# Three accumulation tables in the filter stage, their clearing moved to the setup, and list work of the setup moved

## What is computed

```python
edge_index = jnp.stack([src, dst])
x = _layernorm(x + _L0_gnn_ref(x, edge_index, edge_weight, W, b))            # two hops of normalised sums over edges
x = _layernorm(x + _L1_gnn_ref(x, ..., edge_attr_3, edge_index))             # attention, segment softmax by dst
x = _layernorm(x + _L2_gnn_ref(x, edge_attr_64, src, dst, ...))              # attention, segment softmax by dst
x = _layernorm(x + _L3_gnn_ref(x, edge_attr_20, ..., edge_index))            # filter

def _L3_gnn_ref(x, rbf, Wf1, bf1, Wf2, bf2, Wu1, bu1, Wu2, bu2, gamma, beta, ei):
    row, col = (ei[0], ei[1])                        # row is src: unsorted
    filt = silu(rbf @ Wf1 + bf1) @ Wf2 + bf2
    agg = jax.ops.segment_sum(x[col] * filt, row, num_segments=x.shape[0])
    h = silu(agg @ Wu1 + bu1) @ Wu2 + bu2
    return x + batch_norm(h)                         # over all nodes
```

## Time and profile before

| what | value |
|---|---|
| median of three runs | 7849.68 us (7843.85 to 7850.1) |
| the profiled execution, its own time | 7853.95 us |
| its span | 7852.0 us |
| busy share of the span: PE, DVE, ACT, POOL | 53%, 77%, 46%, 46% |
| bytes moved by DMA, mean rate | 1765 MB, 225 GB/s |
| setup | 0 to 628 us |
| hop 0, hop 1 | 628 to 1150, 1150 to 1681 us |
| layer 0, attention 1, layer 1 | to 2533, to 3610, to 4238 us |
| attention 2, layer 2 | to 4965, to 5602 us |
| filter, update, finish | to 6572, to 7345, to 7852 us |

### The profile page before, as it was taken

How to read it: one execution, slowest core, us unless ns; L and a number is a source line. 1 busy time by engine, 2 the same in 40 slices (tenths; PEclk the granted TensorE clock), 3 DMA queues, 4 the chain that set the end, 5 groups by cost and what they waited for, 6 DMA issues and landing times. The chain is left out here.

```text
span 7852.0 us, 84021 instructions
## 1 busy us (share of the span) xinstructions
PE 4153.3 (53%) x18168; PEld 3161.6 (40%) x18168; DVE 6030.9 (77%) x18094; ACT 3581.2 (46%) x9619; POOL 3600.6 (46%) x3559
## 2 busy tenths in 40 slices
PE   7910000039999333335886222000498998999644
PEld 4500000038888222223554222000266666888522
DVE  7896657767776899998998777899888885554676
ACT  4505750038888333334775000234444443444688
POOL 7806767764443333334555555000266662000477
PEclk9955555569999555557998555555699999999755
DMA  9028989978787566667998888677677776666799
GB/s 285 1 6 236 313 295 298 299 252 243 243 243 227 201 220 220 217 219 249 341 342 276 263 264 264 223 251 252 174 114 115 114 113 147 203 203 204 242 316 304
DMA packets 1120799, 1765.08 MB, mean 225 GB/s; under 512 B 227356, under 2 KB 586372, under 8 KB 1120170
## 3 DMA queue, kind: packets, MB, share of 16 engines
q1 hardware_dynamic: 683786, 1019.20, 40.7%
q0 software_dynamic: 188768, 422.51, 21.9%
q10 hardware_dynamic: 247744, 318.00, 11.7%
HBM read 969.63 MB, written 840.95 MB: 231 GB/s over the span
## 5 line engine op out<-in xcount | busy, mean ns | idle before, releaser
L1125 POOL DMA_INDIRECT rows<-T,index_i x784 | 759.4, 969 | 884.2 <-DVE sums L1267 698.5
L817 ACT ACTIVATE xo<-z,shift,rsd 128x256 f32<-128x256 f32 x1568 | 849.8, 593 | 0.4 <-issue 0.2
L1635 POOL DMA_INDIRECT xt<-X,node_i x392 | 370.8, 946 | 908.4 <-POOLq L1702 784.6
L1386 POOL DMA_INDIRECT A<-comb,ai x392 | 617.6, 1575 | 340.4 <-DMA A<-comb,ai 227.1
L1142 PE MATMUL psE<-encs,attr 4*128 4x256 f32 x784 | 369.7, 649 | 635.5 <-DMA attr<-in_attr3T 633.3
L879 POOL DMA_INDIRECT xt<-in_x,input_i x392 | 375.2, 957 | 470.6 <-DVE xb L894 394.2
L766 PE MATMUL psC<-sums,chainT 128*128 128x256 f32 x4 | 2.4, 700 | 1100.6 <-PEq L655 1100.6
L1401 PE MATMUL psH<-rbf,wf1s 20*128 20x256 f32 x784 | 228.4, 411 | 644.7 <-DMA rbf<-in_rbfT 644.7
L789 DVE BATCH_NORM_STATS2 row_stats<-z 128x6 f32<-128x256 f32 x1568 | 564.5, 402 | 0.1
L1142 PEld LDWEIGHTS psE<-encs,attr 4*128 4x128 f32 x784 | 243.9, 326 | 760.9 <-DMA attr<-in_attr3T 702.2
L801 ACT ACTIVATE sd<-mean_var,epsc 128x2 f32<-128x2 f32 x784 | 237.9, 303 | 584.8 <-DVE mean_var L796 583.0
(11 more groups left out here) (358 smaller groups left out, 14805.5 us busy)
## 6 DMA issues: line engine op xcount, KB each, us to landing
X<-xo ACTq DMA_DIRECT2D x588, 256.0 KB, 3.6
S<-sums SPq DMA_DIRECT2D x196, 544.0 KB, 2.8
st<-S SPq DMA_DIRECT2D x392, 272.0 KB, 4.2
S<-sums SPq DMA_DIRECT2D x392, 256.0 KB, 4.0
A<-zero SPq DMA_DIRECT2D x196, 512.0 KB
T<-tt ACTq DMA_DIRECT2D x196, 280.0 KB
rowsd<-T SPq DMA_DIRECT2D x98, 560.0 KB
T<-tt ACTq DMA_DIRECT2D x196, 272.0 KB
```

The lines of the kernel that those rows point to most:

```text
L817: ins = e.activation(y[s][:, k, :], z[s][:, k, :], ACT.Identity, bias=shift[s][:, k, :], scale=rsd[s][:, k, :])
L1125: e.indirect_dma_start(rows[s][:, k, :], None, table, bass.IndirectOffsetOnAxis(ap=at_i[:, c:c + 1], axis=0))\
L1386: e.indirect_dma_start(A[k], bass.IndirectOffsetOnAxis(ap=ai[s][:, k, :], axis=0), comb[s][:, k, :], None, compute_op=ALU.add).then_inc(si ...
L1635: e.indirect_dma_start(xt[s][:, k, :], None, X3, bass.IndirectOffsetOnAxis(ap=node_i[:, c:c + 1], axis=0))\
```

## The change

What it does, in four parts:

1. A third table A2. The adds of the filter go to A0, A1, A2 in turn by the column's number q, and each waits for add q - 3. `update_nodes` loads all three and adds twice.
2. The attentions no longer store zeros, and wait for none. In block 1 of the setup SP issues, behind the copy to `XT`, 294 stores of zeros (98 for each table, 512 KB each) from a tile `wide_zero` whose rows are 4 KB. At the end of block 4 SP waits for them all.
3. `compress` of the list FREE is cut into pieces and put on DVE between the columns of the histogram, one piece before every 17th column. What it needs is made ahead of the histogram: the scan `frees`, and its sum over earlier partitions by one small product on PE.
4. The shifts to the right of `expand(FREE)`, `input_i`, `head_i`, `tail_i` and `turn_i` are put on DVE in the second hop, one piece after every eighth step for the first twelve. The two fetches of `brow` are at the head of POOL's queue in that hop.

The diff, cut to its core:

```diff
-    A = [dram("A0", NP + P, D), dram("A1", NP + P, D)]
+    A = [dram(f"A{t}", NP + P, D) for t in range(3)]
...
                         e.dma_start(XT[:, 0:D], x.rearrange("p c d -> (p c) d")).then_inc(widened, 16)
+                        for t in A:
+                            for c in range(0, C, QZ):
+                                e.dma_start(nodes(t)[:, c:c + QZ, :], wide_zero[:].rearrange("p (c d) -> p c d", c=QZ)).then_inc(emptied, 16)
...
                         e.memset(zero[:], 0.0).then_inc(zeroed, 1)
+                        e.memset(wide_zero[:], 0.0).then_inc(zeroed, 1)
...
+                        def list_free(t):
+                            if t == 0:
+                                locate(e, link, FREE)
+                                distance(e, link, FREE, notfirst, frees)
+                            elif t <= BITS:
+                                mirror_bit(e, link, BITS - t)
+                            elif t == BITS + 1:
+                                place(e, link, FREE, notfirst)
+                            elif t <= 2 * BITS + 1:
+                                shift_left(e, link, FREE, t - BITS - 2)
+
+                        EVERY = C // (2 * BITS + 3)
...
                         def one_hot(i, s):
+                            if (i * NS + s) % EVERY == EVERY - 1:
+                                list_free((i * NS + s) // EVERY)
...
-                        locate(EMPTY)
-                        locate(FREE)
+                        own(FREE)
+                        locate(e, link, EMPTY)
                         e.sem_inc(located, 1)
-                        compress(FREE, notfirst, frees)
-                        own(FREE)
-                        compress(EMPTY, empty, empties)
+                        distance(e, link, EMPTY, empty, empties)
...
                         join(2)
                         expand(FREE, 2)
-                        link(e.tensor_tensor(ids[:], ids[:], notfirst[:], ALU.mult))
...
                     @block.sync
                     def _(e):
                         e.wait_ge(tabled, 1)
                         e.wait_ge(widened, 16)
                         e.dma_start(nodes(XT)[:, :, D:XW], degs[:]).then_inc(placed, 16)
                         e.wait_ge(placed, 16)
+                        e.wait_ge(emptied, 16 * len(A) * (C // QZ))
...
+                        def list_rows(i, s):
+                            t, rest = divmod(i * NS + s, 8)
+                            if rest == 7 and t < 10:
+                                shift_right(e, link, 9 - t)
+                            elif rest == 7 and t == 10:
+                                inputs_of_rows(e, link)
+                            elif rest == 7 and t == 11:
+                                e.wait_ge(bounded, 32)
+                                turns_of_rows(e, link)
...
-                        unrolled(R, NS, [(mix, 0), (add, 0)] if hop else [(weigh, 0), (square, 0), (weight, 0), (add, 2)])
+                        unrolled(R, NS, [(mix, 0), (add, 0), (list_rows, 0)] if hop else [(weigh, 0), (square, 0), (weight, 0), (add, 2)])
...
-                        written(N, NS, ([(take, 0)] if layer == 1 else []) + [(stage, 0), (store, 2), (empty, 2)])
+                        written(N, NS, ([(take, 0)] if layer == 1 else []) + [(stage, 0), (store, 2)])
...
-                                hold(e, *done(added[k], i, s, 1))
-                                e.indirect_dma_start(A[k], bass.IndirectOffsetOnAxis(ap=ai[s][:, k, :], axis=0), comb[s][:, k, :], None,
-                                                     compute_op=ALU.add).then_inc(signal(added[k], s), 16)
+                                q = (i * NS + s) * G + k
+                                hold(e, *landed(q - len(A)))
+                                e.indirect_dma_start(A[q % len(A)], bass.IndirectOffsetOnAxis(ap=ai[s][:, k, :], axis=0), comb[s][:, k, :], None,
+                                                     compute_op=ALU.add).then_inc(added[q % len(A)], 16)
...
                             e.dma_start(more[s][:], nodes(A[1])[:, c, :]).then_inc(signal(loaded, s), 16)
+                            e.dma_start(third[s][:], nodes(A[2])[:, c, :]).then_inc(signal(loaded, s), 16)
...
                             hold(e, *done(loaded, i, s))
+                            e.tensor_tensor(more[s][:], more[s][:], third[s][:], ALU.add).then_inc(signal(paired, s), 1)
+                            hold(e, *done(paired, i, s))
                             e.tensor_tensor(agg[s][:], agg[s][:], more[s][:], ALU.add).then_inc(signal(summed, s), 1)
```

More of the change, by code:

```diff
@@ L136, in build @@
         isfirst, notfirst, islast, notlast, follows = [sb(n, [P, C]) for n in ("isfirst", "notfirst", "islast", "notlast", "follows")]
+        codes, other, moved = [sb(n, [P, 2, 2 * C]) for n in ("codes", "other", "moved")]
+        rowid, dst_f, brow, carried_r = sb("rowid", [P, C]), sb("dst_f", [P, C]), sb("brow", [P, 2, XW]), sb("carried_r", [P, C])
         head_i, tail_i, start_e = sb("head_i", [P, 1], I32), sb("tail_i", [P, 1], I32), sb("start_e", [P, 1], I32)
@@ L171, in setup @@
                 assert W <= 1024 and C < 512
-                rowid, free, empty, frees, empties = [tmp(n, [P, C]) for n in ("rowid", "free", "empty", "frees", "empties")]
+                empty, frees, empties = [tmp(n, [P, C]) for n in ("empty", "frees", "empties")]
+                EMPTY, FREE, BITS = 0, 1, 10
+                rem, rev, bit, near2, rowsC = tmp("rem", [P, C]), tmp("rev", [P, C]), tmp("bit", [P, C]), tmp("near2", [P, P]), tmp("rowsC", [P, P])
+                pk0, pk1, ck0 = [[tmp(f"{n}{j}", [P, 1]) for j in range(2)] for n in ("pk0", "pk1", "ck0")]
@@ new lines, in setup, with locate @@
+                oh = [[tmp(f"oh{j}{h}", [P, P]) for h in range(2)] for j in range(2)]
+                listed = [tmp(f"listed{j}", [P, W]) for j in range(2)]
+                def locate(e, link, j):
+                    link(e.tensor_scalar(near2[:], rowsC[:], below[:, j:j + 1], None, ALU.is_le))
+                    link(e.tensor_reduce(pk1[j][:], near2[:], AX, ALU.add))
+                    link(e.tensor_scalar(pk0[j][:], pk1[j][:], -1.0, None, ALU.add))
+                    link(e.tensor_scalar(oh[j][0][:], rows0[:], pk0[j][:], None, ALU.is_equal))
+                    link(e.tensor_scalar(oh[j][1][:], rows0[:], pk1[j][:], None, ALU.is_equal))
+                    link(e.scalar_tensor_tensor(ck0[j][:], pk0[j][:], -float(C), below[:, j:j + 1], ALU.mult, ALU.add))
@@ new lines, in place, with shift_left @@
+                def place(e, link, j, flag):
+                    link(e.tensor_scalar(rev[:], rev[:], CODE, 1.0, ALU.mult, ALU.add))
+                    link(e.tensor_tensor(rev[:], rev[:], cols[:], ALU.add))
+                    link(e.memset(listed[j][:, 0:C], 0.0))
+                    link(e.tensor_tensor(listed[j][:, C:W], rev[:], flag[:], ALU.mult))
+                def shift_left(e, link, j, b):
+                    d, top = 2 ** b, CODE * 2 ** (BITS - 1 - b)
+                    a, z = (listed[j][:], other[:, 0, :]) if b % 2 == 0 else (other[:, 0, :], listed[j][:])
+                    e.tensor_scalar(moved[:, 0, :], a, top, 0.0, ALU.subtract, ALU.max)
+                    link(e.scalar_tensor_tensor(z, a, top, a, ALU.is_lt, ALU.mult))
+                    link(e.tensor_tensor(z[:, 0:W - d], z[:, 0:W - d], moved[:, 0, d:W], ALU.add))
@@ L299, in _ @@
                         link(e.tensor_scalar(rowid[:], number[:], OUT, None, ALU.add))
+                        link(e.tensor_scalar(rowsC[:], rows0[:], float(C), None, ALU.mult))
+                        link(e.memset(near[:], 1.0))
+                        link(e.tensor_tensor_scan(frees[:], near[:], notfirst[:], 0.0, ALU.mult, ALU.add))
+                        e.sem_inc(freed, 1)
                         for node, at, to_i, to, off in ((dst_f, col, part_i, part, over),):
@@ L574, in _ @@
                         expand(EMPTY, 1)
+                        for b in reversed(range(BITS)):
+                            shift_right(e, link, b)
+                        identify(e, link, ids)
                         link(e.tensor_tensor(ids[:], ids[:], empty[:], ALU.mult))
@@ L653, in hop_edges @@
                     "weighed", "squared", "weighted", "scaled", "summed"))
-                steps, started = semaphore("steps"), semaphore("started")
+                steps, started, listing, bounded = [semaphore(n) for n in ("steps", "started", "listing", "bounded")]
                 with nc.Block() as block:
@@ L682, in gather @@
                                     .then_inc(signal(gathered, s), 16)
+                        if hop:
+                            for j, c in enumerate((0, C - 1)):
+                                e.indirect_dma_start(brow[:, j, :], None, XT, bass.IndirectOffsetOnAxis(ap=dst_i[:, c:c + 1], axis=0)).then_inc(bounded, 16)
                         unrolled(R, NS, [(gather, 0)])
```

(8 more changed lines are left out.)

162 lines of the change are left out of this document (75 added, 87 removed).

## The result

The change makes the kernel slower: 8079.09 us median of four runs (8073.47 to 8090.09) against 7849.89 (7843.85 to 7852.01) beside it, a ratio of 1.0295 with a 95% interval of 1.0277 to 1.0313. The forecast was 7689, in the other direction. The time lies 7 us from the first rival, 8086.

What follows compares the result with a forecast made beforehand. No engine bounds the whole; stages follow one another. Attention 2 -118, attention 1 -20, filter -78, update +3, hop 1 +7 and setup +45 sum to -161, giving 7689 us, own range 7630 to 7770; range leaving out at most 2 in 10, 7640 to 8090.

Steps and rivals of the forecast that it cites:

- the first rival: SP in block 1: its queue fills, zeros are issued only as fast as moved; 8086 us at 32 deep, chance 0.33.
- Term (a), the end of block 1: Setup: 294 more issues at 0.47 us bring SP to the block's end at 156 us, not 17.7; +105 us.
- The argument that commands and not rows are queued: Block 1, against a filling queue: the copy of 50,176 rows was issued in 0.63 us while its data took 162.
- SP's queue fills: Block 1: SP gets only some transfers ahead, so zeros issue 1.4 us each; 8086 us at 32 deep, chance 0.33.
- the copy holds the queue: Block 1: SP's first store waits for the copy's rows until 182 us, block ends at 320; 7853 us, chance 0.06.
- Filter: Filter: with three tables the wait for landed adds goes, DVE is next at 4.46 us; step 4.80 to 4.4, -78 us.
- Attention 2: Attention 2: without zeros the attributes come sooner, a step falls from 6.7 to 5.5 us; -118 us.
- Attention 1: Attention 1: DVE is the bound and only its waits of 24 us for ACT can go; -20 us.
- Update: Update: a third load and one more addition stay under PE, loads being issued four steps ahead; +3 us, 0 to +25.
- Histogram, FREE, the end of the setup: Setup: list pieces in the histogram +10 us, FREE leaving block 4 -45, DVE's shorter tail at the end -25.
- Hop 1: Hop 1: two fetches ahead of POOL's queue and gathers stretched beside DVE's list pieces; +7 us, 0 to +35.
- the zeros would land in time: Setup's end: zeros land by 580 to 667 us, `XT<-degs` is due at 634; hidden or costing 33, taken as 0.

Runs made afterwards that it cites:

- e7: The change with its zero stores spread over SP's idle time in the setup, the last 26 in attention 1: 7588.9 us, 0.9671 of the kernel before.
- e5: As e7, but with two tables as before the change and no clearing left in attention 1: 7685.04 us, 0.9792 of the kernel before.
- e11: The change with zeros ahead of the copy, which moves to block 2, as 147 stores of 1 MB, 8 KB rows: 7890.5 us, 1.0058 of kernel before.

## Why the prediction was wrong, point by point

**Term (a), the end of block 1: wrong, and it decides.** The step that failed is "294 issues by 0.47 us, SP at 156". It took a duration from stores 6 us apart and multiplied it by 294 for stores in a train. The runs put in its place 160.6 us behind the copy, then 1.285 a store. With the measured +505 for the +105 the forecast would read 7689 + 400 = 8089, against 8079 measured, and e7, which undoes this term alone but for 10 us in attention 1, lies 490 us lower.

**The argument that commands and not rows are queued: wrong.** It read the copy's 0.63 us as the price of the copy. An issue's row ends when the command is handed over; what the command costs SP stands in the row of the next issue. Before the change no issue stood behind the copy, so the row that would have told was not there; the six transfers under way ahead of it in the earlier trace rows were small ones, of 136 KB at most.

**The rivals: right in kind, mispriced in chance.** "SP's queue fills" at 0.33 and "the copy holds the queue" at 0.06 were written as alternatives; they are one mechanism and both acted, and their sum is the result. The range, 7640 to 8090, held it. The point from which it decides (317 us, a depth of 200) was worked out rightly (with the measured gains it is 330), and the prediction had no row for more than seven in flight; with no evidence for 200 the forecast should not have been the likeliest case. The number 8086 was near partly by luck: it took 1.4 us a store where they came 1.285 apart, and a depth of 32 where SP got two or three ahead; the two errors cancel (block 1 at 553 for 555.7).

**Filter: the wait went as forecast, what comes next was read wrong, and the gain is twice the forecast** (-158 for -78, and beyond the bound of -105). The step that failed is "DVE is next, 4.46 us". That was one step out of a stretch in which DVE waited for landed adds 120 times (the waits of e5 are like it), and small operations in it were slow: `cnt` took 0.48 us in that step and 0.17 in its neighbour. The windows of the filter, before and after the change:

```profile
5650.00:6500.00 850.00, 769.55 (x3185) 538.83 (x3184) 711.00 (x2300) 391.20 (x1062) 557.99 (x354) 0.97 0.71 114
```

```profile
6000.00:6700.00 700.00, 700.00 (x3144) 528.54 (x3143) 668.51 (x2267) 385.93 (x1050) 555.95 (x350) 1.00 0.83 137
```

Before, DVE was busy 711 us for 177 steps, 4.0 a step, and so could not need 4.46; POOL's 3.75 lay below. After, 175 steps take 700 us, 4.00 each: PE is busy all of the time and waits for nothing, while DVE works 3.8 us a step. So the profile points to PE, which the prediction did not name here, with DVE close below it; no run separates the two. To find the next bound, take every engine's busy time over many steps, not the distance between two starts in a stretch that stalls.

**Attention 2: right, 20 us too high.** The step was to be 5.5 us and is 5.8. The rows gave 5.65; the 0.15 taken off for the gathers' loss of a competitor did not show. (The floor of 5.3 for DVE's work was too high as well. The window of attention 2 before has 453 us for 92 steps, 4.9 each:)

```profile
4300.00:4920.00 620.00, 172.04 (x736) 163.49 (x736) 453.17 (x1287) 34.38 (x184) 348.29 (x369) 0.50 0.82 263
```

**Attention 1:** right (-25 for -20).

**Update: +40 for +3.** The cover was named (PE, loads four steps ahead) and the queue was not counted: a fourth transfer a step on SP, behind a store that waits for ACT. The step that failed is the term "+3", and DVE's 104 us of waits for the third load stand in its place. The bound of +25 was too low.

**Histogram, FREE, the end of the setup:** right, within 4 and 1 us (for the last two together). **Hop 1:** +17 for +7, inside its range of 0 to 35, and by the stretched gathers that it named. That the zeros would land in time did not come to be tried, as block 1 held everything back; in e7 they did.

## What to carry to other kernels

An issue's own row does not tell what a transfer costs its queue: look at the row of the next issue on the same engine, and where there is none, treat the cost as unknown and as large as the transfer itself. Put long transfers last on an engine that has nothing to do for as long as they move, never ahead of the end of a block in which all engines meet. Before multiplying a duration by a count, ask whether the sample was taken at that density.

## What the runs showed of the hardware that was not expected

- An issue stands until the long command ahead of it is worked off: 160.6 us behind a copy of 50,176 rows of 1 KB, 36.6 behind one of as many rows of 32 bytes, 116 and 125 behind stores of 51.4 MB.
- In a train of stores of 128 rows two are accepted at 0.45 us and, from the fourth on, each at 1.24, for rows of 4 KB and of 8 KB alike. With rows of 8 KB this lasts until some 8 MB are outstanding (an estimate from e11), and from then on the bytes set the pace. Six fills with rows of about 1 KB came at 0.5 us with no hold.
- Rows of 8 KB moved at 419 to 420 GB/s, rows of 4 KB at 406, the copy of 1 KB rows at 320.
- The same program differs by chip: the kernel before takes 7849 us on one and 8068 on another, and the difference lies in hop 0 (some 67 us), the finish (some 97), hop 1 (some 30) and less in others with gathers, while attention 1, with as many gathers, layer 2 and update do not differ.
